# Projection, MLP, norms and last attention batch by batch inside the third cross stage

## The reference

```python
# layers 0 to 2 (16 heads of 8): self-attention, cross-attention, MLP, each with a norm and a residual
# layer 2:
h = ln(x) * (1 + sc_mca) + sh_mca
q = h @ w_q + b_q;  k, v = split(ctx @ w_kv + b_kv)
scores = einsum('bqhd,bkhd->bhqk', q, k) / sqrt(8)
top_s, top_i = top_k(scores, 16)                    # of 1601 keys
attn = softmax(top_s);  o = einsum('bhqk,bhqkd->bqhd', attn, v[top_i])
x = x + (o @ w_co + b_co) * g_mca
h = ln(x) * (1 + sc_mlp) + sh_mlp
u = h @ w_m1 + b_m1;  a, b = u[..., :512], u[..., 512:]
x = x + (silu(a) * b @ w_m2 + b_m2) * g_mlp
# layer 3: one head of 128
nx = ln(x) * gamma + beta
w = softmax((nx @ Wq) @ (ctx @ Wk).T / sqrt(128));  evidence = w @ (ctx @ Wv)
# then a router over 3 experts, the experts, a gate, and the residual, from [nx, evidence, cond]
```

## Time and profile before

| | |
|---|---|
| median of 3 runs | 4852.7 us (4844.91 to 4857.9) |
| the profiled execution's own time, its span | 4842.8 us, 4841.0 us |
| busy in the span: PE, VectorE, ScalarE, GpSimd | 3481.1 (72%), 3584.5 (74%), 2859.6 (59%), 610.9 (13%) |
| granted PE clock, mean of the span | 0.806 |
| third cross stage, first to last pass of the top 16 | 2405.7 to 4210.8 us |
| a batch in it | 225.5 us |

### The profile page before, as it was taken

One profiled execution on the slowest core, in us unless ns is written; L12 is line 12 of the kernel. 1 busy time (PEld: TensorE's weight loads), 2 busy tenths in 40 slices (PEclk: granted clock), 3 DMA queues, 4 the chain that ended last, 5 costly groups with the idle time before them and its releaser, 6 DMA issues. The chain is left out here.

```text
span 4841.0 us, 75811 instructions
## 1 busy us (share of the span) xinstructions
PE 3481.1 (72%) x28020; PEld 1508.0 (31%) x28020; DVE 3584.5 (74%) x5514; ACT 2859.6 (59%) x5351; POOL 610.9 (13%) x1338
## 2 busy tenths in 40 slices
PE   2578999975779999846646656666666655678987
PEld 2222333332223333222222322222232222235553
DVE  6557898926567888525499999999999999732223
ACT  1354888843537888625467777777777776622123
POOL 1121221101333332002110000101010100000000
PEclk7777999987879999977657777777777777789999
DMA  4434434204343433025301111111010100001000
GB/s 132 119 80 101 104 81 93 60 20 127 82 96 89 97 84 76 18 86 98 93 20 38 35 22 34 37 25 37 20 36 20 33 18 8 3 21 34 21 0 9
DMA packets 270015, 267.18 MB, mean 55 GB/s; under 512 B 48977, under 2 KB 238553, under 8 KB 268761
## 3 DMA queue, kind: packets, MB, share of 16 engines
q1 hardware_dynamic: 269656, 262.48, 22.7%
HBM read 152.08 MB, written 109.09 MB: 54 GB/s over the span
## 5 line engine op out<-in xcount | busy, mean ns | idle before, releaser
L1291 ACT ACTIVATE prob<-xa_ps 128x512 f32<-128x512 f32 (+1 forms) x2880 | 1563.8, 598 | 440.6 <-PE xa_ps L1186 417.0
L1378 DVE TENSOR_REDUCE mpart<-ring 128x1 f32<-128x400 f32 (+2 forms) x2816 | 1293.8, 524 | 314.0 <-PE ring L1134 311.1
L1134 PE MATMUL ring<-k_st,q_st 52*128 52x400 bf16 (+2 forms) x3584 | 865.7, 373 | 377.8 <-ACT s_sb L1273 318.2
L1205 PE MATMUL xa_ps<-prob,va 128*16 128x256 f32 (+1 forms) x9984 | 853.8, 425 | 0.5 <-ACT prob L1291 0.5
L1186 PE MATMUL xa_ps<-q_st,k_st 55*128 55x256 bf16 x5504 | 624.7, 301 | 75.1 <-ACT prob L1291 43.8
L1181 PE MATMUL xa_ps<-neg_id,un 128*128 128x128 bf16 (+1 forms) x3328 | 362.4, 275 | 361.6 <-ACT prob L1291 360.0
L1264 ACT ACTIVATE un<-s_sb 128x1601 fp8e4<-128x1601 f32 x256 | 392.7, 1535 | 348.2 <-DVE s_sb L1404 348.2
L1134 PEld LDWEIGHTS ring<-k_st,q_st 52*128 52x128 bf16 x3584 | 254.4, 101 | 904.3 <-ACT s_sb L1273 397.4
L1273 ACT ACTIVATE s_sb<-ring 128x400 f32<-128x400 f32 (+1 forms) x1024 | 472.3, 526 | 34.5 <-PE ring L1134 26.2
L1404 DVE MATCH_REPLACE8 s_sb<-m8b,s_sb 128x1601 f32<-128x1601 f32 x256 | 463.1, 1823 | 0.0
L1397 DVE MATCH_REPLACE8 s_sb<-mpart,s_sb 128x1601 f32<-128x1601 f32 x256 | 463.1, 1823 | 0.0
(11 more groups left out here) (227 smaller groups left out, 3364.8 us busy)
## 6 DMA issues: line engine op xcount, KB each, us to landing
k_st<-kc_dram SPq DMA_DIRECT2D x192, 300.2 KB, 5.3
kc_dram<-k SPq DMA_DIRECT2D x432, 100.0 KB, 2.3
q_st<-q_dram SPq DMA_DIRECT2D x80, 192.0 KB, 3.8
kc_dram<-k SPq DMA_DIRECT2D x144, 100.2 KB, 2.3
ctx_t<-in_ctxT SPq DMA_DIRECT2D x16, 800.5 KB, 5.0
o_dram<-o_sb SPq DMA_DIRECT2D x768, 9.0 KB
q_dram<-pj_q SPq DMA_DIRECT2D x72, 128.0 KB, 2.3
k_dram<-pj_q SPq DMA_DIRECT2D x72, 128.0 KB, 2.3
```

What stands on the lines that cost most here:

```text
L1134: nc.tensor.matmul(ring_ps[:, r % BANKS, 0:w], q_st[rows, b % NQ, 2 * t + pl, qt * P:(qt + 1) * P], k_st[rows, slot_of(n), pl, c0:c0 + w], ...
L1205: last = nc.tensor.matmul(av_ps[32 * k:32 * k + VW, n % 2, :], va[0:sizes[j], b % NVB, j, G * t + k, :], prob[0:sizes[j], s % NPROB, (2 * ...
L1291: nc.scalar.activation(prob[0:size, s % NPROB, hf * 512:(hf + 1) * 512], x_ps[0:size, (2 * s + hf) % XBANKS, :], ACT.Exp, scale=HEAD_SCALE ...
L1378: nc.vector.tensor_reduce(mpart[:, n % 4, row, c:c + 1], ring_ps[:, r % BANKS, 0:chunks[c][1]], AX.X, ALU.max).then_inc(g["red"].sem, 1)
```

## The change

`stage_last` takes the place of layer 2's cross stage and MLP and of layer 3's query and attention. It is the cross stage as before, with further ring items. A batch's further work starts 20 steps after its last unit's steps (`first(b)`), while the next batch's units go on, and is laid out over 58 steps by `LastOrder`: `co` output projection, `mean`, `var` and `bc` of two norms, `m1a` and `m1b` the two halves of the first MLP product, `m2` the second, `q3` the query, `k3` and `v3` keys and values of the last attention, `s3` its score chunks, `t3` its maxima turned, `x3` its 13 steps, `rb` the reciprocal of the denominators spread over the partitions. Items are read by ScalarE (`BY_ACT`) or by VectorE. Residual additions, the diagonals and the split of the maxima are on GpSimd. The work is on 256 columns at a time, one batch. The denominators of the last attention come from two products with one column each instead of one with 256. VectorE does the top 16 in one loop over all pairs, and puts the other work of step k (`between`) ahead of pass `slot(k)`. The ring has 3 banks (4 before) and the exponentials 3 buffers (4 before). The context buffer is used for both layers in turn. The weights' load for layer 3 stands behind the stage; its first three blocks and two vectors are loaded at the stage's start. `VW`, the columns per head in V, is 9 (16 before). Eight semaphore increments in the first load are gone.

```diff
-VW = 16
+VW = 9
...
+        self.end = beside.end if beside else self.last
...
-            upto = min(NU * self.NS, ((k + 1) * self.NS // NT + lead) // 2 * 2)
+            upto = min(NU * self.NS + (turn if beside else 0), ((k + 1) * self.NS // NT + lead) // 2 * 2)
...
+            if beside:
+                mine += beside.items.get(k, [])
...
+class LastOrder:
+    STEPS = NG * CT
+    NF = 4
+
+    def __init__(self):
+        self.items = {}
+        self.sq, self.root, self.shift, self.values, self.top, self.recip, self.out = {}, {}, {}, {}, {}, {}, {}
+        self.end = 0
+        for b in range(B):
+            d = self.first(b)
+            for k in range(4):
+                self.put(self.items, d + k, ("k3", b, k))
+                self.put(self.items, d + 4 + k, ("v3", b, k))
+            self.put(self.items, d, ("co", b))
+            for m, at in ((0, 3), (1, 20)):
+                self.put(self.items, d + at, ("mean", b, m))
+                self.put(self.sq, d + at + 2, (b, m))
+                self.put(self.items, d + at + 3, ("var", b, m))
+                self.put(self.root, d + at + 5, (b, m))
+                self.put(self.items, d + at + 7, ("bc", b, m))
+                self.put(self.shift, d + at + 9, (b, m))
+            for pair in range(2):
+                for kind in ("m1a", "m1b"):
+                    for f in (2 * pair, 2 * pair + 1):
+                        self.put(self.items, d + 13 + pair, (kind, b, f))
+            self.put(self.items, d + 17, ("m2", b))
+            self.put(self.items, d + 30, ("q3", b))
+            for i in range(8):
+                self.put(self.items, d + 31 + i // 2, ("s3", b, i))
+            self.put(self.top, d + 35, b)
+            self.put(self.items, d + 38, ("t3", b))
+            for j in range(CT):
+                self.put(self.items, d + 39 + j, ("x3", b, j))
+                self.put(self.values, d + 41 + j, (b, j))
+            self.put(self.recip, d + 54, b)
+            self.put(self.items, d + 57, ("rb", b))
+            self.put(self.out, d + 58, b)
+            self.end = d + 62
...
+    @classmethod
+    def first(cls, b):
+        return cls.STEPS * (b + 1) + 20
...
+def stage_last(p, nx):
+    BANKS, XBANKS, NPROB = 3, 3, 3
+    LEAD = HQ * NCH + 16
+    plan = Plan(True, NT, NCH, KU, VU, LEAD, 8, order)
+    BY_ACT = ("k", "v", "m", "s", "k3", "v3", "m1a", "q3", "t3", "x3", "rb")
...
+    loads = [("l2", 1), ("l2", 2)]
+    for b in range(B):
+        loads += [("l3", b)] + ([("l2", b + 3)] if b + 3 < B else [])
+    ctx_nth = {what: i + 1 for i, what in enumerate(loads)}
+    ctx_last = {("l2", b): plan.at["v", b, VU - 1] for b in range(1, B)}
+    ctx_last.update({("l3", b): plan.at["v3", b, 3] for b in range(B)})
+    ctx_at = by_step([(plan.v_step(1, VU - 1) + 2, ("l2", 2))] + [(order.first(b) - 7, ("l3", b)) for b in range(B)]
...
+            def x3(r, b, j):
+                if j == 0:
+                    pe.wait_ge(g["rout"].sem, g["rout"].at(nth["t3", b]))
+                ring_free(r)
+                out = ring_ps[0:sizes[j], r % BANKS, 0:T]
+                nc.tensor.matmul(out, kt[:, j * P:j * P + sizes[j]], q_b[:], start=True, stop=False)
+                nc.tensor.matmul(out, ones3[:, 0:sizes[j]], negm[:], start=False, stop=True).then_inc(g["ring"].sem, 1)
+
+            def values3(b, j):
+                if j == 0:
+                    pe.wait_ge(g["rout"].sem, g["rout"].at(nth["v3", b, 3]))
+                    if b == 0:
+                        pe.wait_ge(g["bias"].sem, g["bias"].at(2))
+                    else:
+                        pe.wait_ge(g["ev"].sem, g["ev"].at(b))
+                pe.wait_ge(g["rout"].sem, g["rout"].at(nth["x3", b, j]))
+                pr = prob3[0:sizes[j], j % 2, :]
+                nc.tensor.matmul(av3_ps[:], v3[0:sizes[j], j, :], pr, start=j == 0, stop=j == NT - 1, skip_group_check=True)
+                for h in range(2):
+                    last = nc.tensor.matmul(den3_ps[:, h:h + 1], pr[:, h * P:(h + 1) * P], p.const[0:sizes[j], C_ONES, 0:1], start=False, stop=j == NT - 1, skip_group_check=True)
+                last.then_inc(g["av3"].sem, 1)
...
+            for k in range(STOP):
+                mine = items.get(k, [])
+                if k < END:
+                    x_scores(k)
+                for item in mine[:2]:
+                    ring_item(item)
+                for s in values_at.get(k, []):
+                    values(s)
+                for item in mine[2:]:
+                    ring_item(item)
+                for b, j in order.values.get(k, []):
+                    values3(b, j)
...
+            for k in range(STOP):
+                if k == (NU - 1) * NT - 1:
+                    for q in range(NU * HQ - 4, NU * HQ):
+                        mark(q)
+                if k < END:
+                    expo(k, 0)
+                    expo(k, 1)
+                for n in ocopy_at.get(k, []):
+                    sums_out(n)
+                for b, m in order.sq.get(k, []):
+                    square(b, m)
+                for b, m in order.root.get(k, []):
+                    root(b, m)
+                for b, m in order.shift.get(k, []):
+                    shift(b, m)
+                for item in items.get(k, []):
+                    ring_out(item)
...
+            for k in range(-1, STOP):
+                for n in chain_at.get(k, []):
+                    chain(n)
+                for b, c in split_at.get(k, []):
+                    split_k(b, c)
+                for b in norm_at.get(k, []):
+                    normalise(b)
+                for b, m in order.root.get(k, []):
+                    diagonal(b, m)
+                for b in order.top.get(k, []):
+                    chain3(b)
+                for b in order.recip.get(k, []):
+                    diagonal3(b)
+                for item in items.get(k, []):
+                    if item[0] in ("co", "m2"):
+                        add_res(item[1], 0 if item[0] == "co" else 1, item)
...
+            def between(k):
+
+                for item in items.get(k, []):
+                    if item[0] not in BY_ACT:
+                        side_in(item)
+                for b in recip_at.get(k, []):
+                    recip(b)
+                for b in order.top.get(k, []):
+                    top3(b)
+                for b in order.recip.get(k, []):
+                    recip3(b)
+                for b in order.out.get(k, []):
+                    evidence(b)
+
+            def slot(k):
+                return (k + 1) * NS // NT + LEAD - 10
+
+            at = -1
+            for pair in range(NPAIR):
+                n, i = divmod(pair, HQ // 2)
+                i = (i + 1) * 2 * NCH - 1
+                q, base = 2 * pair, 8 * pair
+                row = place(i)[4] - G
+                if q % HQ == 0 and n >= 4:
+                    dve.wait_ge(g["m"].sem, g["m"].at(n - 3))
+                for k in range(8):
+                    while at + 1 < STOP and slot(at + 1) <= base + k:
+                        at += 1
+                        between(at)
+                    half, sc = k % 2, s_sb[:, (q + k % 2) % 4, :]
+                    best = mpart[:, n % 4, row + G * half, :]
+                    if k < 2:
+                        dve.wait_ge(g["rout"].sem, g["rout"].at(nth["s", n, i - 1 + half]))
+                        ins = nc.vector.max(best, sc)
+                    elif k < 4:
+                        dve.wait_ge(g["chain"].sem, g["chain"].at(base + 1 + half))
+                        ins = nc.vector.match_replace(sc, best, sc, -BIG)
+                    elif k < 6:
+                        dve.wait_ge(g["chain"].sem, g["chain"].at(base + 3 + half))
+                        ins = nc.vector.max(m8b[:, half, :], sc)
+                    else:
+                        dve.wait_ge(g["chain"].sem, g["chain"].at(base + 5 + half))
+                        ins = nc.vector.match_replace(sc, m8b[:, half, :], sc, -BIG)
+                    ins.then_inc(g["chain"].sem, 1)
+            for k in range(at + 1, STOP):
+                between(k)
...
 def program(nc, io):
-            stage_attention(p, layer, "cross")
-            stage_mlp(p, layer)
-        stage_load(p, 3)
+            if layer < 2:
+                stage_attention(p, layer, "cross")
+                stage_mlp(p, layer)
-            stage_query3(p, q, nx)
-            stage_attention3(p, q)
+            nx = p.sb("nx3", [P, TOK], F32, last)
+            stage_last(p, nx)
+            stage_load(p, 3)
             stage_experts(p, nx)
```

806 lines of the change are left out of this document (554 added, 252 removed).

## The result

| | before | after |
|---|---|---|
| median of 3 runs | 4852.7 us (4844.91 to 4857.9) | 4774.95 us (4771.12 to 4776.31) |
| ratio after/before, 95% | | 0.984 [0.982, 0.9859] |
| profiled execution, span | 4842.8, 4841.0 | 4771.1, 4769.0 |
| granted clock over the span | 0.806 | 0.785 |

Faster by 78 us where 189 were forecast: 1.6%, clear of the noise, and 4774.95 lies above the range. I split the span at two events: the first and the last pass of the top 16. Before, they start at 2405.7 and end at 4210.8, 1805.1 us, with 630.2 behind them. After, they run from 2400.4 to 4437.7, 2037.3 us, with 331.3 behind them. The forecast was 134 more between them and 307.5 behind; measured are 232 more and 331.3. So 98 us of the miss lie inside the stage and 24 in the tail; 5 come back since the stage starts earlier, and 6 since the median lies 3.8 above the profiled time and not 9.9.

What follows compares the result with a forecast made beforehand. VectorE's top-16 passes were taken as the bound. Last pass's end 4210.8 + 76 + 58 + 41 + 100 + 166.5 = 4652, or 4664 us at the median's level; range 4590 to 4765.

Steps and rivals of the forecast that it cites:

- 1, VectorE's new work: Inside the stage, side operations add 12 us per batch to VectorE with nothing to hide them, +76 us.
- 3, "it fits if the clock is granted": ScalarE's and PE's added work in the stage stays hidden; cross plus x3 step takes 3.6 of 4.33 us.
- rival B: PE bounds the x3 steps if its clock stays at half: 4830 us, 4750 at a clock between; chance 0.14.
- 2, waits for the ring: VectorE in the stage waits for late ring chunks, 9 us per batch (0 to 30), +58 us.
- 4, the tail: Behind VectorE's last pass: 41 us to the last unit's sums, 100 for batches 6 and 7, 166.5 for load and experts.
- 5, at nothing: VW, removed semaphore marks, context transfers, three exponential buffers and GpSimd's additions were priced at no cost.
- Rival A: ScalarE's function table switches cost double, 10 us more per batch, half becoming VectorE waits: 4699 us; chance 0.06.
- C: All ring waits in the stage hidden, 0 to 2 us per batch: 4610 us; chance 0.10.
- D: VectorE and the ring lock in step, slower than before, 5054 us at two passes per side step; chance 0.08.

Runs made afterwards that it cites:

- e5_off7: e1_wide with VectorE's side work placed 7 chunks behind the ring's head instead of 10; 4645.74 us, ratio 0.9576.
- e9_colplace: The changed kernel, one-column denominators kept, with VectorE's side work 7 chunks behind the ring's head instead of 10; 4711.29 us, ratio 0.9729.
- e1_wide: The changed kernel with the last attention's denominators back as one product of 256 columns, and a 128x256 reciprocal on VectorE; 4701.92 us, ratio 0.9684.
- e3_small: The kernel before with 3 ring banks and 3 exponential buffers instead of 4 each in its third cross stage; 4846.1 us, ratio 0.9988.
- e8_notable: e1_wide without function table switches: Silu became Identity and Sqrt became Copy, changing the computation; 4675.09 us, ratio 0.9641.
- e2_col: The kernel before with its last attention's denominators as two one-column products, exponentials stationary, instead of one of 256 columns; 4958.25 us, ratio 1.0228.
- e10_128: The kernel before with its last attention's denominators as two products of 128 columns each, exponentials stationary; 4845.57 us, ratio 1.0004.

## Why the prediction was wrong, by its steps

*1, VectorE's new work: right, a little high.* VectorE is busy 1868.6 us between first and last pass, 63.5 more than the 1805.1 before; 76 was forecast. 12.5 less.

*3, "it fits if the clock is granted": the failed step.* The pace of 1.70 us per x3 step was read from the earlier trace rows, where the denominators have 256 columns, and used for a step in which they have one. The clock wasn't granted. Alone, in the tail, the step took 3.18 at 0.50; among the cross steps the clock was 0.58 to 0.78, and PE came late out of each batch's x3 steps, with VectorE idle for 5 to 15 us in each of the six stretches. This is rival B; I gave it 0.14, and held against it that PE has no pause in the last attention and "these steps have hardly one". In the tail they had none, and it didn't help. Its price was put at 26 us per batch; the 17.3 seen in one batch are form and place together. At its middle, 4750, B stands 86 us above my forecast, against the 73 that putting the form back gives: that size is near. But B spoke of the clock alone and didn't name the form of the denominators, and the other 38 us of the miss aren't in it. Putting the form back gives 73 us: 51.5 of VectorE's idle time less 9 of longer reciprocals in the stage, 32 in the tail.

*2, waits for the ring: mechanism right, size half.* With the form put back, VectorE is still idle 117.2 us in the stage where 58 was forecast, 94 of it in front of side work. I took 9 us per batch, between 0 and 30; it was 18 in all, 15 of them in front of side work. That they come from the place in VectorE's order, as the step says, is shown by e5_off7 and e9_colplace: three passes later they are gone; the masks' part in it is seen in one case, in time at 3570.53. That the place could be moved, I didn't ask. The rows of e1_wide say which steps I mis-sized. The gate products waited 22.9 us, where 2.9 per batch make 19, and the maxima 11.0, where 2.8 make 18. The out-projection alone took 24.3 in 7 batches, 3.5 each, where I had 2.2 for it with the first mean and variance; and the two norms took 30.0 us (9.8 for the subtractions, 7.8 for the variances, 12.4 for the scalings, to which I had given nothing).

*4, the tail: right but for the same step.* To the last unit's sums 37 us (41 forecast), load and experts 164 (166.5). The two runs of 13 x3 steps took 3.18 us per step for 1.70, 38 us more in all (2 x 13 x 1.48), against 14 that came in under the forecast elsewhere. With the wide form the tail is 299.6, under the 307.5 forecast.

*5, at nothing: right.* e3_small shows it for the smaller buffers. But the form of the denominators should have been on the list of what changes.

*Rival A* falls by its rows (gaps of 0.02 us before and 0.03 after, at the loads shown) and by e8_notable's 21 to 27 us, where twice the price would have given up to twice the 40. The drain stated by the Trainium skill, ScalarE: Activation LUTs (What ACT_TABLE_LOAD costs), isn't seen in any of the 16 loads in front of a square root, whose group has 0.3 us of idle time in all:

```profile
L2018 ACT ACT_TABLE_LOAD x16 | 20.5, 1283 | 0.3
```

*C* and *D* did not come.

The sum, made good: the miss of 111 is 110.7 more of idle time in the stage (168.7 - 58), less 12.5 of item 1, 23.8 more of tail, less 5 and 6 for the start and the level. The form of the denominators is 73 of it by experiment. The rest, 38, is the size of item 2 (59 more idle time in e1_wide than forecast) less what came in under the forecast there: 8 in the tail, 4 of VectorE's new work, 1 for the start and 9 for the level.

## What to carry over

A duration may be taken from a trace only for an instruction of the same form: compare not only how many products a step has but which operand is the stationary one and how many columns move. Then ask what an edit does to its neighbours: in e2_col the products that weren't edited paid for the one that was. And where work is merged into a bound engine's order, its place is a number to be swept: here one number was worth 52 to 71 us, where the change itself gave 78.

## What the runs showed of the hardware

- A TensorE that the profile shows without a pause can stay at its lower level (1.2 GHz): busy 39.00 of 39 us at 0.50 in after. With 128 columns in place of one in the same instructions the last attention is granted the upper level (2.4 GHz) nearly all the time, 0.95 in e10_128 (0.96 before), where e2_col was granted 0.66 (4400 to 4700):

```profile
4340.00:4675.00 335.00, 303.81 (x1361) 191.27 (x1360) 77.34 (x181) 72.05 (x163) 0.00 (x0) 0.95 0.06 20
```

  The Trainium skill, TensorE: Matmul & The Clock Gate (Why this matters for your kernels), gives as the recipe for the full clock to keep TensorE busy without a break. By the busy time of the profile these traces don't agree: it was busy 39.00 of 39 us, and the clock stayed low. The ends of products are modelled in the profile, so this busy time doesn't say how full the engine was.
- The instructions alone don't fix the level: e2_col's batches run the same ones in the same order, six in 3.18 us per step and two in 1.72. One of the six starts at the upper level (two products of 256 columns in 0.70 us at 4664.68) and is at the lower one at 4667.89 (1.20 us), with no idle time of PE between.
- One column instead of 128 saves nothing per step. The means of 295 and 284 ns in the groups above mix the two levels; at the upper level alone a one-column product took 229 ns (e2_col's fifth batch) and one of 128 columns 274 (e10_128's third), yet the step is 1.72 us in both:

```profile
L1689 PE MATMUL a_den<-const,a_prob 128*128 128x1 f32 x44 | 5.5, 229 | 0.0
```

```profile
L1689 PE MATMUL a_den<-const,a_prob 128*128 128x128 f32 x44 | 6.7, 274 | 0.0
```

- A reciprocal of 128x256 takes VectorE 1.74 us, four times its product of the same size (0.42).
